# Steps of all phases placed anew, two GpSimd biases behind VectorE, whole tiles in the opening (macaron layer, one core)

## The reference, cut to what matters

```
x = x + 0.5 * ffn(layernorm(x))     # ffn: relu(x @ Wq1.T + b1) @ Wq2.T + b2, weights quantised to -1, 0, 1
x = x + attn(layernorm(x))          # 16 heads of 8 channels, rotary q and k, softmax, values, Wo
x = x + 0.5 * ffn(layernorm(x))     # the same ffn
```

## Time and profile before

| | us |
|---|---|
| median of 3 runs | 520.1 (518.65 to 523.45) |
| the profiled execution | 519.27 |
| its span, first to last instruction | 517.5 |
| PE busy | 488.3 (94%) |
| VectorE busy | 409.2 (79%) |
| ScalarE busy | 347.5 (67%) |
| GpSimd busy | 203.5 (39%) |

### The profile page before, as it was taken

The page is one execution under the profiler, slowest core; times in us unless marked ns, Lnnn a source line. Parts: engine busy times, 40 slices in busy tenths (PEclk is TensorE's granted clock), DMA queues, the critical chain, the costliest instruction groups (busy, mean ns, idle before and its releaser), DMA issues.

```text
span 517.5 us, 13169 instructions
## 1 busy us (share of the span) xinstructions
PE 488.3 (94%) x5455; PEld 227.2 (44%) x5455; DVE 409.2 (79%) x644; ACT 347.5 (67%) x429; POOL 203.5 (39%) x226
## 2 busy tenths in 40 slices
PE   6689999899999999999999999999999999998996
PEld 3455435252354535363354533443344334443445
DVE  5776997958998689877897699779987998898124
ACT  5627565757767687577867677766776778578841
POOL 3507065707338080825534183336342650005001
PEclk8998999999999999999999999999999999999999
DMA  8047037203350136203450147024612451000000
GB/s 276 25 163 166 11 120 208 42 4 123 124 125 3 40 125 177 56 3 97 171 125 4 45 146 189 16 63 162 148 23 56 156 149 36 23 3 3 3 22 20
DMA packets 20007, 44.63 MB, mean 86 GB/s; under 512 B 2860, under 2 KB 5420, under 8 KB 18924
## 3 DMA queue, kind: packets, MB, share of 16 engines
q1 hardware_dynamic: 18636, 41.96, 28.4%
q10 hardware_dynamic: 1312, 1.84, 1.0%
HBM read 20.58 MB, written 18.87 MB: 76 GB/s over the span
## 4 chain that ended last, share of the span: by engine, by line
PE 72%; DVE 15%; ACT 6%; issue 3%; DMA 2%; POOL 1%; ACTq 0%; DVEq 0%; POOLq 0%
PE heads_acc L577 19%; PE side L584 18%; PE unit L560 14%; PE unit L541 12%; DVE maxima L906 8%; ACT probs L788 3%; ACT hidden L778 3%; PE side L621 2%; PE side L611 1%; DMA q_scratch<-q_parts 1%; PE heads_acc L652 1%; PE side L606 1%; PE unit L584 1%; DVE stats_ffn L873 1%; DMA resid<-in_x 1%
## 5 line engine op out<-in xcount | busy, mean ns | idle before, releaser
L906 DVE TENSOR_REDUCE maxima<-unit 128x2 f32<-128x1024 f32 x256 | 304.7, 1219 | 57.3 <-PE unit L541 56.4
L788 ACT ACTIVATE probs<-unit 128x1024 f32<-128x1024 f32 x256 | 256.2, 1025 | 99.1 <-PE unit L560 98.2
L577 PE MATMUL heads_acc<-probs,v_heads 128*32 128x512 f32 x1024 | 135.3, 601 | 0.6 <-ACT probs L788 0.4
L560 PE MATMUL unit<-q_stack,k_stack 64*128 64x512 f32 x512 | 118.7, 463 | 5.9 <-DVE maxima L906 5.3
L541 PE MATMUL unit<-k_stack,q_stack 62*128 62x512 f32 x512 | 114.0, 442 | 2.5 <-DVE maxima L906 1.0
L560 PEld LDWEIGHTS unit<-q_stack,k_stack 64*128 64x128 f32 x512 | 47.6, 184 | 72.6 <-DVE maxima L906 33.9
L541 PEld LDWEIGHTS unit<-k_stack,q_stack 62*128 62x128 f32 x512 | 48.3, 185 | 61.9 <-ACT probs L788 30.6
L584 PE MATMUL side<-w_q,hidden 128*32 128x128 f32 x1664 | 53.5, 275 | 0.0
L386 POOL TENSOR_TENSOR rope_a_k<-k,cos_t 128x512 f32<-128x512 f32 x7 | 8.9, 1277 | 101.6 <-ACT k L775 101.6
L584 PEld LDWEIGHTS side<-w_q,hidden 128*32 128x32 f32 x1664 | 43.2, 110 | 12.4 <-issue 8.9
L1062 POOL TENSOR_SCALAR var_eps_ffn<-mean_var_ffn 128x4 f32<-128x4 f32 x15 | 3.7, 249 | 108.1 <-DVE mean_var_ffn L877 108.1
(11 more groups left out here) (144 smaller groups left out, 461.0 us busy)
## 6 DMA issues: line engine op xcount, KB each, us to landing
k_scratch<-k_parts SPq DMA_DIRECT2D x16, 512.0 KB, 2.9
q_scratch<-q_parts SPq DMA_DIRECT2D x14, 512.0 KB, 3.3
k_stack<-k_scratch SPq DMA_DIRECT2D x16, 384.0 KB, 5.4
q_stack<-q_scratch SPq DMA_DIRECT2D x16, 384.0 KB, 6.8
resid<-in_x SPq DMA_DIRECT2D x8, 256.0 KB, 4.8
k_stack<-k_scratch SPq DMA_DIRECT2D x16, 128.0 KB, 2.5
k_swap<-k SPq DMA_DIRECT2D x14, 128.0 KB, 2.3
q_swap<-q SPq DMA_DIRECT2D x14, 128.0 KB, 2.3
```

Source lines behind the costliest of these rows:

```text
L560: mm = pe.matmul(to[:, e, :], k_stack[part, quad // NQ % 2, pair, kt * P:(kt + 1) * P], q_stack[part, quad // NQ % 2, pair, :], start=True ...
L577: mm = pe.matmul(heads_acc[32 * j:32 * j + 32, :], v_heads[:, b % 2, at, ODD * odd:ODD * odd + 32], probs[:, burst % RING, j, :], start=(k ...
L788: act.activation(probs[:, burst % RING, 2 * pp:2 * pp + 2, :], unit_of(PLACE["exp", n]), ACT.Exp, scale=SCALE).then_inc(s_exp, 1)
L906: dve.tensor_reduce(maxima[:, quad % 2, :, r], unit_of(PLACE["max", k]), AX_X, ALU.max).then_inc(s_max, 1)
```

## The change

Three things are changed, and no instruction is added to or taken from the work except waits and the cut of tiles:

- All three lists are written anew, with the same words in other places. SyncE now takes the store of the batch before, the first row of maxima of the next batch and the two swaps in the order in which the lists have `ffn2_down3`, `max_T4`, `k` and `q`; before, it was store, row, k, q.
- Two of GpSimd's `add_bias` wait for VectorE: the one of ffn1, batch 1, until VectorE has applied the attention norm of batch 0, and the last one until VectorE has applied the last norm.
- `column_tiles` takes a width. In `PROLOGUE` it is 128, so `up`, `down` and `v` there are whole tiles; in the batches, and for the `down` steps between the first eight "m", it stays 32.

```diff
@@ -56,27 +56,27 @@
 
 
 FIRST = [
-    "e m fill1", "e m first_max_T1", "e m m fill2 attn_T@1", "e m m fill2 k@1", "e m m q@1", "e m m ffn1_T@3",
-    "e m pv m max_T1", "e m pv m ffn1_up0@3", "e m pv ffn1_up1@3", "e m pv ffn1_up2@3", "e m ffn1_up3@3",
-    "e m pv max_T2 ffn1_stats", "e m ffn1_down0@3 ffn1_down1@3", "e pv m ffn1_down2@3 ffn1_down3@3 ", "e m", "e pv m v",
-    "e m attn_stats ffn1_T", "e m pv", "e m heads_copy0 ffn1_up0", "e m max_T3 ffn1_stats@5", "e pv m ffn1_up1",
-    "e m heads_T0 pv", "e m ffn1_up2 ffn1_up3", "e m pv ffn1_down0", "e m ffn1_down1 ffn1_down2 ffn1_down3", "e m pv",
-    "e m max_T4", "e pv m attn_T", "e m k", "e pv m", "e m q", "e m pv",
+    "e m fill1", "e first_max_T1 m", "e m m fill2 attn_T@1", "e m m k@1 fill2", "e m m", "e q@1 m m ffn1_T@3",
+    "e m pv m max_T1", "e pv m m m ffn1_up0@3", "e pv ffn1_up1@3", "e m pv ffn1_up2@3", "e m ffn1_up3@3",
+    "e m pv max_T2 ffn1_stats", "e", "e pv ffn1_down0@3 ffn1_down1@3 m ffn1_down2@3 m", "e ffn1_down3@3 m", "e m v",
+    "e m pv attn_stats ffn1_T", "e m pv", "e m heads_copy0 ffn1_up0", "e m pv max_T3 ffn1_stats@5 pv", "e m ffn1_up1 m",
+    "e heads_T0", "e m ffn1_up2 ffn1_up3 m", "e pv ffn1_down0 ffn1_down1", "e m ffn1_down2 ffn1_down3", "e m",
+    "e pv m m max_T4", "e pv attn_T", "e m k", "e pv m", "e m q", "e m pv",
 ]
 STEADY = [
-    "e m ffn1_T", "e m", "e pv m heads_copy1@-1 ffn1_up0", "e m pv max_T1", "e m", "e heads_T1@-1 pv m", "e m pv",
-    "e m out_T", "e m ffn1_stats@5 ffn1_up1", "e m", "e ffn1_up2 pv m", "e m ffn1_up3 pv max_T2", "e m", "e out m",
-    "e m ffn1_down0", "e m ffn1_down1 attn_stats ffn2_stats", "e m", "e ffn1_down2 ffn1_down3 pv m", "e pv m",
-    "e m max_T3 pv heads_copy0 ffn2_T", "e pv heads_T0 m", "e m ffn2_up0 pv ffn2_up1", "e m", "e v m", "e pv ffn2_up2 m",
-    "e m ffn2_up3 pv attn_T", "e m", "e ffn2_down0 ffn2_down1 m", "e m ffn2_down2 ffn2_down3", "e m", "e pv max_T4 m",
-    "e m k pv q pv",
+    "e m ffn1_T", "e pv heads_copy1@-1 m", "e m ffn1_up0 pv", "e heads_T1@-1 m", "e m max_T1 pv ffn1_up1",
+    "e m out_T attn_stats", "e m", "e out pv m", "e m ffn1_up2 pv", "e m ffn1_up3", "e m pv max_T2", "e m ffn2_stats",
+    "e ffn1_down0 ffn1_down1 m", "e m ffn1_down2 ffn1_down3", "e m", "e v m", "e m ffn2_T pv", "e m", "e pv ffn2_up0 m",
+    "e m pv max_T3 ffn1_stats@5 heads_copy0", "e m ffn2_up1 pv", "e m ffn2_up2 pv pv ffn2_up3", "e m",
+    "e ffn2_down0 ffn2_down1 m", "e m ffn2_down2 ffn2_down3", "e m", "e pv attn_T m", "e m max_T4 pv", "e m k", "e m",
+    "e heads_T0 pv m", "e m q pv",
 ]
 LATER = [
-    "e m", "e pv m heads_copy1@-1", "e m heads_T1@-1", "e pv m", "e m pv max_T1", "e m out_T", "e m out", "e m pv",
-    "e ffn2_stats m", "e pv m v", "e m", "e pv max_T2 m", "e m ffn2_T", "e m pv", "e m ffn2_up0",
-    "e m attn_stats ffn2_up1", "e m", "e ffn2_up2 pv m", "e m ffn2_up3 pv heads_copy0", "e m max_T3 pv", "e m",
-    "e attn_T pv m", "e m ffn2_down0", "e m ffn2_down1", "e m", "e ffn2_down2 m", "e ffn2_down3 pv m",
-    "e m max_T4 pv pv k", "e m", "e pv m", "e q m", "e m pv heads_T0",
+    "e m", "e pv m heads_copy1@-1", "e m pv", "e max_T1 m", "e m heads_T1@-1", "e m pv", "e m out_T", "e m out", "e m pv",
+    "e ffn2_stats m", "e pv pv m", "e v m", "e m pv max_T2", "e m ffn2_T", "e m pv ffn2_up0", "e m attn_stats ffn2_up1",
+    "e m ffn2_up2", "e m pv heads_copy0 ffn2_up3", "e m", "e pv max_T3 m", "e m attn_T", "e m k", "e m",
+    "e pv heads_T0 m", "e m pv q", "e m", "e pv pv max_T4 m", "e m ffn2_down0 ffn2_down1", "e m", "e ffn2_down2 m",
+    "e pv m", "e m pv ffn2_down3",
 ]
 
 PLANS = [FIRST if b == 0 else STEADY if b + AHEAD["ffn1"] < B else LATER for b in range(B)]
@@ -508,14 +508,15 @@
                     stack(b + 1, slice(2, NPAIR), s_stack[(b + 1) % 2])
                 if b < B:
                     max_row(b * NQ + 3)
-                if 0 < b < B:
-                    sp.wait_ge(s_y, b)
-                    sp.dma_start(out[b - 1].rearrange("(p t) d -> p t d", t=T), batch_rows(b - 1)).then_inc(s_stored, 16)
-                if on("values", b):
-                    max_row((b + 1) * NQ)
-                if on("proj", b):
-                    swap("k", b + 2)
-                    swap("q", b + 2)
+
+                for word in " ".join(PLANS[b]).split() if b < B else ():
+                    if word == "ffn2_down3" and b > 0:
+                        sp.wait_ge(s_y, b)
+                        sp.dma_start(out[b - 1].rearrange("(p t) d -> p t d", t=T), batch_rows(b - 1)).then_inc(s_stored, 16)
+                    elif word == "max_T4" and on("values", b):
+                        max_row((b + 1) * NQ)
+                    elif word in ("k", "q") and on("proj", b):
+                        swap(word, b + 2)
             for h, ts in enumerate(ends):
                 sp.wait_ge(s_end_y, h + 1)
                 sp.dma_start(out[last].rearrange("(p t) d -> p t d", t=T)[:, ts, :], batch_rows(last)[:, ts, :]).then_inc(s_stored, 16)
@@ -578,17 +579,16 @@
-            def column_tiles(to, lhs, rhs, start, stop):
-
-                for c in range(0, P, TILE_COLS):
-                    mm = pe.matmul(to[c:c + TILE_COLS, :], lhs[:, c:c + TILE_COLS], rhs, start=start, stop=stop)
+            def column_tiles(width, to, lhs, rhs, start, stop):
+
+                for c in range(0, P, width):
+                    mm = pe.matmul(to[c:c + width, :], lhs[:, c:c + width], rhs, start=start, stop=stop)
-            def side_work(use):
-                if use is None:
-                    return
+            def side_work(use, width=TILE_COLS):
+
...
@@ -622,7 +622,7 @@
-                    column_tiles(to, w_proj[:, "qk".index(name), :], x_T[:], True, True).then_inc(s_qk_psum[name], 1)
+                    column_tiles(width, to, w_proj[:, "qk".index(name), :], x_T[:], True, True).then_inc(s_qk_psum[name], 1)
...
@@ -630,18 +630,18 @@
-                        mm = column_tiles(to[:, t * P:(t + 1) * P], lhs[:, t * P:(t + 1) * P], w_proj[:, w, :], True, True)
+                        mm = column_tiles(width, to[:, t * P:(t + 1) * P], lhs[:, t * P:(t + 1) * P], w_proj[:, w, :], True, True)
-                        mm = column_tiles(to, w1_q[:, arg * P:(arg + 1) * P], part[:], n == 0, n == 1)
+                        mm = column_tiles(width, to, w1_q[:, arg * P:(arg + 1) * P], part[:], n == 0, n == 1)
-                        mm = column_tiles(to[:, arg * P:(arg + 1) * P], hidden[:, n, arg * P:(arg + 1) * P], w2_q[:, n, :],
+                        mm = column_tiles(width, to[:, arg * P:(arg + 1) * P], hidden[:, n, arg * P:(arg + 1) * P], w2_q[:, n, :],
...
@@ -667,7 +667,7 @@
                 if use[0] == "v":
                     pe.wait_ge(s_late, 16 * LATE_CONST_DMAS)
                 fill(FILL.get(use[:3], 0))
-                side_work(use)
+                side_work(use, P)
             fill(FILL_BEFORE_MAX)
             pe.wait_ge(s_rows_fill[0], ROWS_FILLED)
             for k in range(OPEN_MAX):
@@ -1084,6 +1084,8 @@
             add_bias("ffn1", 0)
             ln_rstd("ffn1", 2)
             ln_rstd("attn", 0)
+
+            pool.wait_ge(s_normed["attn"], T)
             add_bias("ffn1", 1)
             ln_rstd("attn", 1)
             ln_apply(pool, "attn", 1)
@@ -1135,6 +1137,7 @@
                 pool.tensor_tensor(rstd["ffn2"][:, ts], var_eps["ffn2"][:, ts], minus_half[:, ts], ALU.pow).then_inc(s_end_rstd, 1)
             pool.wait_ge(s_end_x2, 2)
             pool.wait_ge(s_y, last)
+            pool.wait_ge(s_end_normed, T)
             pool.tensor_tensor(xb["ffn2"][:], batch_rows(last), b2_half[:].to_broadcast([P, T, D]), ALU.add).then_inc(s_end_xb, 1)
 
 
```

## The result

The changed kernel takes 524.1 us (median of 17 runs, 519.6 to 528.0) against 519.1 for the kernel before beside it: ratio 1.0071 (95% interval 1.0047 to 1.0094). A second set of runs gave 1.0061 (1.0025 to 1.0097). The ratios leave out executions in a slower state (among these 17, 528.0 and 527.6 of the changed kernel, and 585.2 of the one before) and are not quotients of the medians, which would give 1.010 here and 1.005 in the second set. By the ratios the changed kernel is 0.6 to 0.7% slower, where 510.7 us was forecast. The profiled execution took 520.49 us, its span is 518.7, 1.2 us longer than before.

A forecast was written before the change was run, and what follows sets the result against it. A batch was taken as bounded by VectorE's sum up to the worst step plus TensorE's after it. Terms -0.56, -0.94, -0.1, -3.9, -3.2 and -0.7 summed to -9.4; from 519.27 that gave 509.9, plus 0.8: 510.7 us, range 503.5 to 519.5.

The forecast's parts named there:

- the one on GpSimd and the splits: LATER's earlier k and q move GpSimd's ropes between splits of maxima: zero taken, -3 to +3 us.
- STEADY, -1.3 a batch: New list in the three STEADY batches: 1.3 us less each from 58.1, -3.9 in all.
- floor of 56.4: Least time of a STEADY batch: TensorE's sum of 54.7 us plus 1.7 of its own small waits.
- rule of turns: Each batch takes at least VectorE's sum up to a step plus TensorE's after it, for the worst step.
- hand-offs that I had charged 0.4 for: STEADY steps 3 to 5, side bank: heads_T to max_T and up1 to out_T get tighter, 0.4 us between them.
- LATER, -0.8 a batch: New list in the four LATER batches: 0.8 us less each, -3.2 in all, bounds -0.5 and -1.6 a batch.
- My 51.7: Time expected for a LATER batch between first scores with the new list, in us.
- FIRST, -0.7: New list in batch 0: VectorE and TensorE taking turns sum to 67.0 us against 67.7, so -0.7.
- GpSimd's waits: Bias moved behind VectorE's norms: -0.56 us in the opening and -0.94 at the end.
- Whole tiles, -0.1: Opening with whole instead of column tiles: one entry less on the path, -0.1 us, bounds -0.5 and +1.0.
- SyncE's queue, zero: New order of stores, maxima rows and swaps: transfers hidden, zero, up to +0.5 us a LATER batch.
- ScalarE's turn in LATER: Slower rival, chance 0.10: ScalarE becomes the turn after VectorE in steps 12 to 22, total about 528 us.

The follow-up runs named there:

- The fills: Changed kernel with idle products laid into TensorE's waits in batches 3, 4, 5 and 6: 521.0 us, ratio 1.0002.
- the fastest kernel: Changed kernel with three added GpSimd waits keeping it off the splits, and the LATER list of before in batches 6 and 7: 508.1 us, ratio 0.9772.

## Why the prediction was wrong

**The step that failed** is the one on GpSimd and the splits: "I take zero, with -3 to +3 us". I had the mechanism, the right instruction and the right move ("moves GpSimd's ropes off the split of step 1 and perhaps onto that of step 25"), and priced it by the mean, 0.24 a split. A mean over 31 splits says little of a split that decides: where the transpose is next in PE's queue, the price is both halves held, (1.23 - 0.18) + (1.19 - 0.18) = 2.1 us, of which 1.87 reached TensorE. The row for it was there, 1208 ns as the longest half. The rule of the Trainium skill that I had cited (SBUF — State Buffer, SBUF: two separate sides) says that one of the two engines holds the shared ports "for the whole instruction". The trace agrees to 0.04 us in each of the pairs above. By that rule the walk through GpSimd's queue from k's new step would have given the collision, and I didn't make it. The term also looked at k and q in LATER alone: what q's rotation and the biases hold in the STEADY batches (1.1 to 1.3 us each) and in step 3 of batch 4 (1.8) was in no term.

**What it cost.** Changed kernel against the one with free splits, by profiles: 1.3, 1.1 and 1.1 us in batches 1 to 3, 3.5 in batch 4 and 1.8 in batch 5; in batch 6 1.5, where the clock fell. That is 10.3 of the 11.1 us between the spans; the rest is in the opening. By medians it is 13 (523.0 against 510.0 beside each other).

**The clock** was in no step of the prediction. The fills showed that the falls behind the new waits cost another 3 us or so of the usual run (ratio 1.0071, and 1.0061 in the repeat, against 1.0002 with fills).

**STEADY, -1.3 a batch:** measured -1.6, -1.3 and -0.3 with splits held, and -1.4, -1.8 and -1.3 with both kernels' splits free. The size was right, but partly by luck: the 58.1 us from which it started held 0.7 us of held splits (57.4 as a mean once they are free), and the floor of 56.4 was wrong, 55.9 measured. The rule of turns fits these numbers; no run tests it alone. The hand-offs that I had charged 0.4 for, heads_T to max_T and up1 to out_T, show 0.26 and 0.19 over their steps.

**LATER, -0.8 a batch:** wrong beyond the lock. With splits free the new list gives 51.63 us in batches 4 and 5, against 51.87 and 51.68: -0.2 and -0.05. My 51.7 for it came true only because the 52.5 from which I started held 0.75 us of a held split in step 3 (batch 5 takes 51.7 with the old list once it is free). And I took all four batches as equal: batch 6 has no attn_T, k or q, so that steps 20 to 25 of the new list are nearly scores alone, 1.0, 0.7 and 0.7 over in the first three. The new list costs 1.6 there.

**FIRST, -0.7:** nothing. Batch 0 took 67.3 to 67.5 with either list: steps 2, 6 and 22 are 1.17, 1.11 and 1.42 over in the new one, waits that my sum of turns didn't hold. The old list waits about as long in steps 2 and 22.

**GpSimd's waits:** -0.56 in the opening, 0.7 measured at full clock; in the changed kernel's profile x_T came at 26.92, not at 26.06, since the clock of 16.3 to 26.1 us was 0.83 there. -0.94 at the end: 0.60 us instead of 1.54, right. **Whole tiles, -0.1:** -1.1 in the transfer of q's parts, outside my bound of -0.5 and in a place that the prediction didn't look at; about -1.4 by medians in the fastest kernel, and nothing in the time of the run in which they stood by themselves. **SyncE's queue, zero:** the steps in which a new row of maxima is first read are at most about 0.3 over. **ScalarE's turn in LATER:** steps 12 to 22 of batches 4 and 5 are 0.4 over at most, so the slower rival didn't occur; the loss came from an engine that it didn't name.

That the changed kernel takes 510.0 us once GpSimd is kept off the splits, where 510.7 was forecast, is luck: it is another kernel, and the errors cancel (LATER and FIRST gave less than I took, free splits and tiles more).

## What to carry to other kernels

When work moves between steps, follow it to the engine that nobody lists: write down when each GpSimd instruction will run, and look which short VectorE instructions with a reader right behind them fall beside it. A 0.17 us instruction can then last 1.2 us, and one semaphore wait on GpSimd, which had time to spare (39% busy), was worth more than three lists placed anew (ratio 1.007 or 1.006 to 0.991, falls of the clock included, against 3.2 us). Price such a collision by its longest row at the place where it decides, not by its mean, and give the batches that lack part of the work their own list.

## What the hardware did that I hadn't expected

- VectorE's split (16 numbers a partition, from SBUF to SBUF) was held until the end of the GpSimd instruction beside it, within 0.04 us, up to 1.27 us for 0.17.
- Waits of 0.7 to 2 us in mid-run were followed in some executions by stretches of 3.4 or 6.8 us at 1.2 GHz (four of them in one profile of the changed kernel, one in the other) and in others not: in the first profile neither step 26 brought one. With idle products in those waits the runs' clocks were 0.984 to 0.997, against 0.974 to 0.993 without, and the waits were as long.
- The times scatter less without held splits, as far as few runs can tell: by 7.5 us in ten runs of the changed kernel, by 4.0 in six with free splits and 0.7 in five with the old last list as well; the kernel before, with few held splits, scattered by 4.7 beside them. That the falls of the clock are the reason isn't tested.
- The transfer of q's parts in the opening took 1.1 us more in each of the five profiles in which a transfer on the instruction queue was under way as it began.
